# The last of four row tiles: two 512-wide projections computed in three terms of rounded parts instead of in full fp32

## The reference

```python
x = x + L0_xattn(layernorm(x), ctx)      # 16 heads of 32; weights (x+1 or 1/(1-x)) / sum, no softmax
x = x + L0_attn(layernorm(x))            # 8 query heads of 64, one K and one V; causal softmax, then @ Wp + bp
x = x + L0_ffn(layernorm(x))             # 2 shared experts (mean) + top 2 of 8 routed experts, gelu
```

## Time and profile before

| what | value |
|---|---|
| median of 3 runs | 1218.68 us (1218.37 to 1218.9) |
| the profiled execution: its time | 1217.79 us |
| the profiled execution: its span | 1216.1 us, mean granted TensorE clock 0.998 |
| TensorE matmul busy | 1201.8 us (99%) |
| VectorE, ScalarE, GpSimd busy | 840.1, 685.9 and 570.8 us |

### The profile page before, as it was taken

How to read it: one execution, slowest core, us unless ns; L and a number is a source line. 1 busy time by engine, 2 the same in 40 slices (tenths; PEclk the granted TensorE clock), 3 DMA queues, 4 the chain that set the end, 5 groups by cost and what they waited for, 6 DMA issues and landing times.

```text
span 1216.1 us, 33732 instructions
## 1 busy us (share of the span) xinstructions
PE 1201.8 (99%) x14478; PEld 1127.3 (93%) x14478; DVE 840.1 (69%) x1224; ACT 685.9 (56%) x1236; POOL 570.8 (47%) x357
## 2 busy tenths in 40 slices
PE   9999999999999999999999998999999999999998
PEld 8899999999999999999999997988889999999997
DVE  7767776786876886876876859666765455655655
ACT  5266656755756656656756567455553455444453
POOL 5756767776867776867767664000041010000000
PEclk9999999999999999999999999999999999999999
DMA  8331111121121122121122135654556699999991
GB/s 293 102 111 37 41 41 37 44 90 54 44 81 57 59 71 75 38 84 42 41 71 76 56 133 195 257 208 147 180 176 227 226 354 338 341 343 362 362 367 37
DMA packets 34794, 179.39 MB, mean 148 GB/s; under 512 B 6265, under 2 KB 9497, under 8 KB 15569
## 3 DMA queue, kind: packets, MB, share of 16 engines
q1 hardware_dynamic: 32896, 172.42, 38.7%
q0 software_dynamic: 1744, 4.76, 1.2%
HBM read 168.97 MB, written 8.19 MB: 146 GB/s over the span
## 4 chain that ended last, share of the span: by engine, by line
PE 95%; DVE 2%; ACT 1%; DMA 1%; issue 1%; SPq 0%; POOL 0%; DVEq 0%
PE bank L926 20%; PE bank L929 20%; PE bank L1283 12%; PE sc L1300 9%; PE sc L949 8%; PE sc L1144 7%; PE bank L968 4%; PE sc L1164 4%; PE bank L1164 4%; PE bank L1035 1%; DMA tt<-in_wv 1%; PE bank L1089 1%; PE bank L994 1%; PE sc L1105 1%; DVE xres L1765 0%
## 5 line engine op out<-in xcount | busy, mean ns | idle before, releaser
L729 POOL TENSOR_TENSOR xn<-xn,tt 128x1024 f32<-128x1024 f32 x96 | 230.6, 2402 | 143.0 <-DVE tt L1621 141.0
L929 PE MATMUL bank<-wvh,blk 128*128 128x256 f32 x1344 | 246.8, 286 | 0.0
L926 PE MATMUL bank<-blk,wkh 128*128 128x256 f32 x1344 | 245.9, 285 | 0.0
L1719 DVE TENSOR_TENSOR wsl<-ring,wsh 128x2048 fp32r<-128x2048 f32 x72 | 168.6, 2341 | 111.4 <-ACT wsh L1376 108.7
L1440 ACT ACTIVATE tt<-sc 128x512 f32<-128x512 f32 (+1 forms) x208 | 107.8, 602 | 212.4 <-PE sc L949 212.4
L926 PEld LDWEIGHTS bank<-blk,wkh 128*128 128x128 f32 x1344 | 209.2, 192 | 4.2 <-issue 1.6
L929 PEld LDWEIGHTS bank<-wvh,blk 128*128 128x128 f32 x1344 | 208.8, 191 | 2.6
L926 PE MATMUL bank<-blk,wkl 128*128 128x256 f32 x672 | 190.0, 283 | 0.0
L929 PE MATMUL bank<-wvl,blk 128*128 128x256 f32 x672 | 189.9, 283 | 0.0
L1376 ACT CAST wsh<-ring 128x2048 fp32r<-128x2048 f32 x72 | 137.4, 1909 | 45.0 <-PE sc L1300 21.2
L1283 PEld LDWEIGHTS bank<-xT,ring 128*128 128x128 f32 x1280 | 144.8, 192 | 1.0
(11 more groups left out here) (326 smaller groups left out, 2196.1 us busy)
## 6 DMA issues: line engine op xcount, KB each, us to landing
ring<-in_w SPq DMA_DIRECT2D x112, 1024.0 KB, 5.8
stg<-in_ctx SPq DMA_DIRECT2D x24, 1024.0 KB, 5.0
wqt<-in_wo SPq DMA_DIRECT2D x4, 1024.0 KB, 5.2
wqt<-in_aq SPq DMA_DIRECT2D x4, 1024.0 KB, 5.6
wqt<-in_ap_ SPq DMA_DIRECT2D x4, 1024.0 KB, 5.1
yrows<-K SPq DMA_DIRECT2D x1, 2048.0 KB, 12.5
bsum<-in_tails SPq DMA_DIRECT2D x2, 520.0 KB, 6.8
ktail<-bsum SPq DMA_DIRECT2D x1, 1040.0 KB, 5.9
```

The source lines that it names most:

```text
L729: e.tensor_tensor(dacc[0:kn, y, :], dacc[0:kn, y, :], tt[0:kn, w, :], ALU.add).then_inc(s["da_pool"], 1)
L926: m = e.matmul(dst[:, 256 * a:256 * a + 256], w[:, WPOS[j], c, r], x[:, c, :], start=(k_ == 0), stop=(k_ == 5))
L929: m = e.matmul(dst[:, 256 * a:256 * a + 256], x[:, c, r], w[:, WPOS[j], c, :], start=(k_ == 0), stop=(k_ == 5))
L1719: e.tensor_tensor(wsl[m % 3][:], ring[slot(unit_split(m))][:], wsh[m % 3][:].bitcast(F32), ALU.subtract).then_inc(s["wl_dve"], 1)
```

## The change

Tile 3 takes the path of the other three tiles. The branches for `t == 3` and for the last two batches are gone, and with them `cT` and `oT`. `halved` gives two more slots, 98 and 111, at which ScalarE casts the weights of tile 3, and GpSimd takes their low parts: the first at slot 99 of its loop, the second after its loop, between `biased(3)` and the iota.

```diff
 def normalised_by(b):
-    return 4 * min(b + 1, NB - 2) + 2 * max(b - (NB - 3), 0)
+    return 4 * (b + 1)

 def halved(slot, what):
-    return next((t for t in range(3) if slot == (slot_of(t, 0) - 5, slot_of(t, 5))[what]), None)
+    return next((t for t in range(4) if slot == ((NCH - 6, slot_of(3, 3) + 2) if t == 3 else
+                                                 (slot_of(t, 0) - 5, slot_of(t, 5))[what]), None)
...
-        Q2 = oT = xa
+        Q2 = xa
...
-        cT = xT[:, 2, :].rearrange("p (g q) -> p g q", g=4)
...
             biased(3)
+            output_weights_lo(3, 1)
             e.wait_ge(s["wo_pe"], 4)
             e.iota(iotaw, pattern=[[1, D]], base=0, channel_multiplier=0).then_inc(s["wide_pool"], 1)
...
             def output(t):
                 dst = take("w", t)
                 e.wait_ge(s["cr_dve"], normalised_by(2 * t + 1))
-                if t == 3:
-                    e.wait_ge(s["wo_in"], 64)
+                e.wait_ge(s["wol_pool"], 2 * t + 1)
+                for x_, (c_, w_) in enumerate(((cTh, woh), (cTh, wol), (cTl, woh))):
                     for g in range(4):
-                        m = e.matmul(dst[:], cT[:, g, :], wot[:, g, :], start=(g == 0), stop=(g == 3))
-                else:
...
+                        m = e.matmul(dst[:], c_[:, g, :], w_[:, g, :], start=(x_ == 0 and g == 0),
+                                     stop=(x_ == 2 and g == 3))
...
             def self_output(t):
                 dst = take("pr", t)
                 wait_read(e, "o", t, 1)
-                if t == 3:
-                    e.wait_ge(s["ap_in"], 64)
+                e.wait_ge(s["wol_pool"], 2 * t + 2)
+                for x_, (o_, w_) in enumerate(((oTh, woh), (oTh, wol), (oTl, woh))):
                     for hp in range(4):
-                        m = e.matmul(dst[:], oT[:, P * hp:P * hp + P], wqt[:, hp, :], start=(hp == 0), stop=(hp == 3))
-                else:
...
+                        m = e.matmul(dst[:], o_[:, P * hp:P * hp + P], w_[:, hp, :], start=(x_ == 0 and hp == 0),
+                                     stop=(x_ == 2 and hp == 3))
...
             def attended(t, b):
-                ov = oT[:].rearrange("p (h b t) -> p h b t", h=4, b=2)
...
-                if t == 3:
-                    e.tensor_copy(ov[:, :, b, :], src).then_inc(read_of("o", t, b), 1)
-                else:
...
+                e.tensor_copy(hv, src).then_inc(s["oh_dve"], 1)
+                e.wait_ge(s["oh_dve"], 2 * t + b + 1)
+                e.tensor_tensor(lv, src, hv.bitcast(F32), ALU.subtract).then_inc(read_of("o", t, b), 1)
...
                 qs = slice(64 * y, 64 * y + 64)
-                if b >= NB - 2:
-                    e.tensor_tensor(cT[:, :, qs], cU[:, y, :, :], bvt[:], ALU.add).then_inc(s["cr_dve"], 1)
-                    return
                 e.tensor_tensor(cU[:, y, :, :], cU[:, y, :, :], bvt[:], ALU.add).then_inc(s["cr_dve"], 1)
```

More of the change, by code:

```diff
@@ L113, in normalised_by @@
 def normalised_by(b):
-    return 4 * min(b + 1, NB - 2) + 2 * max(b - (NB - 3), 0)
+    return 4 * (b + 1)
 def halved(slot, what):
-    return next((t for t in range(3) if slot == (slot_of(t, 0) - 5, slot_of(t, 5))[what]), None)
+    return next((t for t in range(4) if slot == ((NCH - 6, slot_of(3, 3) + 2) if t == 3 else
+                                                 (slot_of(t, 0) - 5, slot_of(t, 5)))[what]), None)
 def slot_of(t, d):
@@ L1684, in attended @@
             def attended(t, b):
-                ov = oT[:].rearrange("p (h b t) -> p h b t", h=4, b=2)
                 e.wait_ge(s["o_pe"], 2 * t + b + 1)
                 src = pj_of("o", t, b)[:, 0:256].rearrange("p (h t) -> p h t", h=4)
-                if t == 3:
-                    e.tensor_copy(ov[:, :, b, :], src).then_inc(read_of("o", t, b), 1)
-                else:
[L1691 to L1695, removed]
+                hv = oTh[:].rearrange("p (h b t) -> p h b t", h=4, b=2)[:, :, b, :]
+                lv = oTl[:].rearrange("p (h b t) -> p h b t", h=4, b=2)[:, :, b, :]
+                e.tensor_copy(hv, src).then_inc(s["oh_dve"], 1)
+                e.wait_ge(s["oh_dve"], 2 * t + b + 1)
+                e.tensor_tensor(lv, src, hv.bitcast(F32), ALU.subtract).then_inc(read_of("o", t, b), 1)
             def self_output(t):
```

## The result

The change measures 1220.46 us (median of 22 runs, 1218.43 to 1221.48) against 1218.19 us for the kernel before (22 runs, 1217.27 to 1220.74); the ratio is 1.0016, 95% interval 1.0010 to 1.0021. That is 1.9 us slower (1.2 to 2.6). It lies mostly inside the 0.2% that I called no difference, but the interval does not reach 1: with 22 runs of each kernel the loss is resolved. The profiled execution took 1220.42 us, its span 1218.7 us, 2.6 us longer than before.

The account below looks back on a forecast made before the run. TensorE, busy 1201.8 of 1216.1 us, was taken as the bound, through its queue and waits. The terms -0.2 + 2.2 - 0.7 gave +1.3 us; 1.4 on the 1218.68 us median made 1220.1 us, range 1217.8 to 1221.7.

Parts of the forecast that it names:

- The product: TensorE, both projections: 12 matmuls take 2.73 us instead of 3.43, so each gets 0.7 us shorter.
- First projection's weights: ScalarE's cast at slot 98 and GpSimd's 4.6 us subtraction at slot 99 fit idle time: cost 0.
- First projection's rows: VectorE's added work delays what is queued behind by 0.8 us, so `shared_up(4)` keeps 0.2 us of the 0.7 gained.
- Second projection's weights: Late load and cast, then GpSimd's 4.6 us subtraction holds VectorE before `shared_down(7)` and the transposition: 2.2 us lost.
- my upper bound of 2.6: Second projection's weights: loss of 2.6 us if the low parts of unit 8 also end late.
- The bound of 0.7 us: Second projection's weights: loss of only 0.7 us if GpSimd can hold a VectorE operation for just 2 us.
- Second projection's rows: Two added VectorE subtractions, 0.85 us together, are done more than 1.5 us before TensorE reaches the projection.
- `hidden(11)` just in time: Behind the second projection, its chain carries the 2.2 us delay, not the gain, and uses up 0.7 us to spare.
- Sum: Whole kernel: -0.2 + 2.2 - 0.7 = +1.3 us, 1.1 to 1.6 with rounding; 1.4 added to the median.
- Rival C: New TensorE idle time around `shared_down(7)` lowers the clock once, adding 1.6 us: 1221.7 us; chance 0.15.
- Rival B: Both projections' gains kept, VectorE not held or with more slack: -1.4 us, 1217.3 us; chance 0.12.
- Rival A: Second projection's weights land by 797.5, transposition 1.0 us late: sum +0.1, 1218.8 us; chance 0.22.

Follow-up runs that it names:

- `w_only`: The change with only the first projection in three terms, the second left in full fp32: 1217.65 against 1218.55 us for the kernel before, ratio 0.9991.
- `no_low`: The change without GpSimd's low part of the second projection's weights, that term left out of the result: 1191.27 us, ratio 0.9771 to the kernel before, with fewer routed blocks.
- `after_2`: The change profiled a second time, unaltered: 1220.24 us in a single run.
- `load_only`: The change with the second projection's weight load put ahead of ring unit 15, cast still at slot 111: 1219.40 against 1218.68 us for the kernel before, ratio 1.0004.
- `pr_only`: The change with only the second projection in three terms, the first left in full fp32: 1221.12 against 1218.55 us for the kernel before, ratio 1.0018.
- `early`: The change with the second weight load ahead of ring unit 15 and its cast at slot 110: ratio 0.9987, then 0.9990, to the kernel before.
- `quarters`: The change with GpSimd's second subtraction written as four instructions of a quarter each: 1219.29 against 1218.68 us for the kernel before, ratio 1.0009.

## Why the prediction was right

1220.1 us was forecast and 1220.46 measured, and the mechanism is the one forecast. That the two times are within 0.4 us is in part luck: I added 1.4 us (the sum of the steps is 1.3) to a median of three runs, 1218.68 us, and over 22 runs the kernel before has 1218.19. The difference was forecast as 1.4 us and measured as 1.9. By steps:

- **The product, 0.7 us each.** 0.62 us each: 3.43 to 2.80 and 2.81. I had taken the 12 matmuls of a `shared_down`, 2.73 us; near enough.
- **First projection's weights, 0.** Right. GpSimd ran them from 724.62 for 4.63 us and had 1.82 us to spare before the next sum at 731.07.
- **First projection's rows.** The cast and the subtraction came at 756.50 and 756.83 and moved all behind them by 0.74 us, as forecast; the low part of unit 4 started at 770.09 instead of 769.40. But what it costs TensorE was mis-sized: I left 0.2 us of the gain. I had TensorE's place from one execution, and by chance from that with the shortest stretch at the low clock, 4.32 us for the `shared_down` ahead of the projection. That stretch moves TensorE's rows and not VectorE's. Of the eight profiled executions with the change's first half, the two with 4.62 us (`w_only`) and 4.66 us (`no_low`) show the wait at `shared_up(4)`, 2.96 and 2.95 us, and lose 0.1 us; the six with 4.75 us and more, both of the change among them, show 2.85 or 2.86. With 4.32 us the loss would be about 0.4 us and 0.2 us would be left, an estimate. In the profiles of the change 0.6 us was kept.
- **Second projection's weights, 2.2 us lost.** The mechanism was right in every link: landing 8.1 us after the issue, cast ending at 801.2 (800.8 forecast), L1661 held to the end of GpSimd's instruction, `shared_down(7)`, the exponentials, the transposition. The size was 2.8 us, above my upper bound of 2.6. Two terms were missing. `hidden(7)` began at 805.79 and took 0.84 us instead of 0.43, and I put that down to the iota that stands right behind the subtraction on GpSimd (805.81 to 806.35). I had written that nothing asks for the iota, which is true, and not that it may hold something. No run moved the iota by itself, but L1715 ends 0.28 us behind it here, in `after_2` and in `load_only` alike, as it ends 0.3 us behind the subtraction in `pr_only` and `early`; and in `no_low`, with no GpSimd instruction there, it takes 0.43 us. And a group that starts after a gap takes longer than one that follows another: 3.04 us instead of 2.73 for `shared_down(7)`, 0.63 instead of 0.43 for the transposition, a part of the 2.8 us that the wait itself does not show. All other traces agree: 3.02 to 3.04 us for `shared_down(7)` wherever it waited, 0.63 us for the transposition wherever it came late.
- **The bound of 0.7 us**, a hold of 2 us at most, is out: the holds were 4.2 us (change) and 3.4 us (`early`).
- **Second projection's rows, 0**, and `hidden(11)` just in time: the latter was late by 0.2 us (2.91 us for that `shared_down`, 2.73 before).
- **Sum.** -0.6 + 2.8 - 0.6 + 0.2 = +1.8 us; the ratio gives +1.9 us (1.2 to 2.6). In my +1.4 the gain of the first projection was too small by 0.4 us and the loss of the second by 0.6, and the two errors cancelled in part.

**Rival C** is not the usual case. Neither profiled execution of the change shows it. Five of its 22 runs have a mean granted clock of 0.995 and a median of 1221.33 us, the 15 at 0.997 have 1220.23 us, and `quarters` shows that a fall behind such a wait can cost 1.5 us. But the kernel before has such runs too: of the 26 beside `quarters` three are at 0.995, with 1219.88 to 1220.88 us against a median of 1218.68. So it is open whether any of the five runs is this mechanism. **Rival B** falls with the holds. **Rival A** was right as a mechanism: its kernel loses 1.7 us in the stretch before the product's gain, where I had written 1.0; the iota and the starts after a gap are missing there too.

## What to carry to other kernels

Work moved to an idle GpSimd is not free by GpSimd's idle time. Look at what VectorE has queued there that works on SBUF alone, and whether it has slack for the whole length of one GpSimd instruction; small operations count as much as long ones. A copy out of PSUM was not held: L1583, at 727.67 in the middle of the first subtraction, took 0.69 us as before. Cutting the instruction into pieces shortens each hold but lengthens the work; moving it by one slot was worth more (+1.1 against -1.2 us). Before adding a consumer to a load, look at what the load stands behind in its queue: here it stood behind a ring unit and its wait, and only the load issued 6.7 us earlier, landing at 791.3, made the slot before usable.

## What the runs showed of the hardware that I had not expected

- The hold goes both ways. GpSimd's four pieces, a quarter of 4.6 us each, took 7.78 us beside VectorE, and the whole subtraction in `load_only` took 4.93 us instead of 4.61, where it met a VectorE subtraction in its first 0.4 us (798.23 to 800.52).
- GpSimd's iota, which reads no tensor, seems to hold a VectorE operation as well (L1715, 0.84 us instead of 0.43), and is itself longer where it met L1715 already at work: 0.79 us in `pr_only` and `early`, 0.56 in the kernel before. The argument is in the timings above; no run tests it alone.
- One wait of 2.0 us between busy stretches was followed, in the profiled execution of `quarters`, by some 3.4 us at a granted clock of 0.50 (1.2 GHz). The waits of 2.2 us in the two profiled executions of the change, of 2.0 us in `pr_only` and of 1.0 us in `no_low` and `load_only` were not: the clock stayed at 1.00. Nor is it bound to the change's gap: in the same profile the clock was at 0.50 from 89 to 92 us, and in `early`, where TensorE is busy for the same 18.4 of the 20 us from 80 us on, it stayed at 1.00.
